# Sparse mixture with TensorE three and six steps behind its row turning

## The chip, the core and the metric

The program runs on one NeuronCore of a Trainium2 chip. Engines are called PE (TensorE matmul; PEld its weight loads), DVE (VectorE), ACT (ScalarE), POOL (GpSimd) and SP (SyncE, which here issues DMAs). The metric is the device time of one execution in microseconds; the median of three runs of the kernel before is 885.31 us (885.22 to 888.61).

## The reference

Two layers of gated cross attention and a gated mixture of experts on 128 x 64 tokens of 128 numbers. The change touches the last mixture alone:

```
h  = layernorm(x)                       # 8192 tokens x 128
i, p = top 2 of 8 experts by h @ Wg     # softmax over the two
out = x + tanh(g) * sum over the two:  p * ((silu(h @ W1[i]) * (h @ W2[i])) @ W3[i])
```

W1 and W2 are 128 x 256, W3 is 256 x 128, for each of 8 experts; all in float32.

## The kernel before

The first phase does the first layer's attention. The second goes in groups of 512 tokens through the first mixture, the second attention and the routing; POOL scatters each normalised row with its share and place to its expert's region in DRAM (`sorted_rows`). The sparse mixture then runs over 135 tiles (`DTILES`) of 128 sorted rows, all of one expert. Its first steps are mixed with the last two groups of the routing, by an order written out by hand.

Each engine has a function `sparse(t)` for step t. No planner sets the order: every engine runs its instructions in the order of the code, and semaphores hold it.

- PE, step t: the first products of tile m = t - HIDDEN (four 128 x 128 products against W1 and W2, line 1938, each float32 product two matmul records), the turning of tile t (line 1948), the output of tile w = t - OUT (two products, line 1957). One signal, `ends_mm`, is given at the end of the step, and `hidden_mm` after the first products.
- ACT, step t: copies the tile's W1 and W2 (`w12`, line 1708) to one of three buffers, then Silu of tile t - HIDDEN (line 1714).
- DVE, step t, once `ends_mm` says that PE's step t is over: the gating product h of tile t - HIDDEN (line 1446, waits for Silu), the copy of the turned tile t to `xT` (line 1451), its two last columns (1452), the share of tile t - OUT (1462), the copy of W3 (1468). From step 86 it also adds 56 pieces of finished groups to X (line 1483).
- POOL, from step 11 on: one indirect DMA for each tile's share (line 1202), each held back until PE's `ends_mm` of a step that the code counts out. Before and between them come the paced scatters of the last two groups' rows (line 1186).
- SP loads the tiles' rows seven ahead (`ROWS`), and later pairs of contributions.

HIDDEN is 2 and OUT is 4. PSUM has eight banks; the first products use banks 0 and 1 in turn, the turned tile bank 3 (from tile 17 on also bank 4), the output banks 5 and 2. So PE's step t needs DVE's step t - 2: its first products wait for `xT` of tile t - 2, which DVE copies after the gating product of tile t - 4.

Of the kernel before, what the change touches and what calls it, by code (L numbers as in the profile page):

```python
# [5 lines left out]
ALU = mybir.AluOpType  # L6
# [7 lines left out]
P = 128  # L14
# [965 lines left out]
def mixtures_and_attention(nc, sb, psum, sem, c, a, X, dispatch, out):  # L980
# [71 lines left out]
    HIDDEN, OUT = 2, 4  # L1052
# [3 lines left out]
    xT = [sb(f"d_xT{i}", [D, P], F32) for i in range(4)]  # L1056
    w12 = [sb(f"d_w12_{i}", [D, 2 * HID1], F32) for i in range(3)]
# [25 lines left out]
    PIECES_AT, FIND_AT = 86, 30  # L1083

    def pair_step(g):
        return 87 + 7 * g // 2
# [7 lines left out]
    found = pair[0:1, 0, 0:2 * LATE_TILES].rearrange("p (k n) -> p k n", k=2)  # L1094
# [19 lines left out]
    with nc.Block() as block:  # L1114
# [115 lines left out]
        def _(dve):  # L1230
# [208 lines left out]
            def sparse(t):  # L1439


                dve.wait_ge(ends_mm, t + 1)
                m = t - HIDDEN
                if 0 <= m < DTILES:
                    dve.wait_ge(silu_done, m + 1)
                    dve.tensor_tensor(d_hidden[m % 4].rearrange("p k n -> p (k n)"), silu[m % 2],  # L1446
                                      uv[m % 2][:, KH * P:2 * KH * P], ALU.mult).then_inc(h_ready, 1)
                if t < DTILES:
                    if t >= 4:
                        dve.wait_ge(hidden_mm, t - 3)  # L1450
                    dve.tensor_copy(xT[t % 4][:], tr_bank(t)[:, 0:P]).then_inc(d_xT_ready, 1)  # L1451
                    dve.tensor_copy(ends[:, t % KEEP, :], rows[t % ROWS][:, D:ROW]).then_inc(row_read, 1)
                w = t - OUT
                if w >= 0:
                    dve.wait_ge(row_read, w + 1)
                    if w % 4 == 0:
                        here = slice(w % KEEP, w % KEEP + min(4, DTILES - w))
                        if w >= KEEP:
                            dve.wait_ge(kept[w // 4 % 8], 64 * (w // KEEP))
                        dve.wait_ge(row_read, min(w + 4, DTILES))  # L1460
                        dve.tensor_copy(token[:, here], ends[:, here, 0])
                    dve.tensor_scalar(shares[w % KEEP], y_bank[w % 2][:, 0:D], ends[:, w % KEEP, 1:2], None,  # L1462
                                      ALU.mult).then_inc(share_ready, 1)
# [118 lines left out]
            for t in range(17, DTILES + OUT):  # L1582
                if t - 18 < dispatch.LATE_STEPS and t >= 18:
                    dispatch.plan_late(dve, c, t - 18, found)
                if t == FIND_AT + 2:
                    dispatch.plan_late(dve, c, dispatch.LATE_STEPS, found)
# [5 lines left out]
        def _(act):  # L1592
# [106 lines left out]
            def sparse(t):  # L1699


                if t < DTILES:
# [3 lines left out]
                    if t >= 3:  # L1706
                        act.wait_ge(hidden_mm, t - 2)
                    act.copy(w12[t % 3][:], c.w12[:, bass.ds(experts[t % 4], 1)].rearrange("d a i h -> d (a i h)")).then_inc(w12_ready, 1)  # L1708
                m = t - HIDDEN
                if m >= 0:  # L1710
                    act.wait_ge(hidden_mm, m + 1)
                    if m >= 2:
                        act.wait_ge(h_ready, m - 1)
                    act.activation(silu[m % 2], uv[m % 2][:, 0:KH * P], ACT.Silu).then_inc(silu_done, 1)  # L1714
# [59 lines left out]
        def _(pe):  # L1774
# [151 lines left out]
            def sparse(t):  # L1926


                m, w = t - HIDDEN, t - OUT
                if 0 <= m < DTILES:  # L1930
                    pe.wait_ge(d_xT_ready, m + 1)
                    pe.wait_ge(w12_ready, m + 1)
                    if m >= 2:
                        pe.wait_ge(h_ready, m - 1)
                    else:
                        pe.wait_ge(k_ready if m == 0 else weighted_ready[0], G)
                    for i in range(2 * KH):
                        last = pe.matmul(uv[m % 2][:, bass.ts(i, P)], w12[m % 3][:, bass.ts(i, P)], xT[m % 4][:], start=True, stop=True)  # L1938
                    last.then_inc(hidden_mm, 1)
                if t < DTILES:  # L1940
# [3 lines left out]
                    elif t == 17:  # L1944
                        pe.wait_ge(next_row_done, G)
                    else:
                        pe.wait_ge(d_xT_ready, t if t <= 16 else t - 1)
                    last = pe.transpose(tr_bank(t)[:, 0:P], rows[t % ROWS][:, 0:D], c.ident[:])  # L1948
                if w >= 0:
                    pe.wait_ge(h_ready, w + 1)  # L1950
                    pe.wait_ge(w3_ready, w + 1)
                    if w >= 2:
                        pe.wait_ge(share_ready, w - 1)
                    else:
                        pe.wait_ge(q_ready if w == 0 else chosen_ready, G - w)
                    for k in range(KH):
                        last = pe.matmul(y_bank[w % 2][:, 0:D], d_hidden[w % 4][:, k, :], w3[w % 8][:, bass.ts(k, D)],  # L1957
# [50 lines left out]
            for t in range(15, DTILES + OUT):  # L2008
                if t == FIND_AT:
                    dispatch.find_late(pe, c, found)  # L2010
# [93 lines left out]
```

## Time and profile before

| what | us |
|---|---|
| median of three runs | 885.31 |
| the profiled execution | 885.49 |
| its span in the profile | 883.7 |
| first to last turning of the sparse mixture | 593.8 to 865.1 |
| last share computed | 871.0 |

PE is busy 766.4 us of the span (87%), DVE 679.8 (77%), ACT 562.8 (64%), POOL 462.4 (52%). These are means over phases with different limits. The sparse mixture takes some 271 us, so it is read by itself: how many matmuls a stretch holds, which waits stand before them, and what the other engines do in those waits. The ends of matmul records are modelled, so a wait of another engine for PE is read from when that other engine starts.

### The profile page before, as it was taken

How to read it: one execution, taken by the hardware profiler on the slowest of the kernel's cores; microseconds unless marked ns; L12 is line 12 of the kernel's file. 1: busy time of each engine (PE TensorE's matmuls, PEld its weight loads, DVE VectorE, ACT ScalarE, POOL GpSimd, SP SyncE). 2: the span in 40 equal slices, each digit the busy share in tenths (PEclk: the TensorE clock that was granted, in tenths of full speed). 3: DMA queues.
4: the chain of work that ended last, by engine and by line, in shares of the span. 5: the costliest groups of instructions: out<-in, count | busy, mean ns of one | idle time of the engine just before them, and what ended most of it. 6: DMA issues, size and time to landing. Idle time of an engine off the chain costs nothing. (4 is left out here: it accounts for less than half of the span.)

```text
span 883.7 us, 26192 instructions
## 1 busy us (share of the span) xinstructions
PE 766.4 (87%) x8321; PEld 589.6 (67%) x8321; DVE 679.8 (77%) x2969; ACT 562.8 (64%) x1195; POOL 462.4 (52%) x498
## 2 busy tenths in 40 slices
PE   4899999999999979989989988757888888889983
PEld 2566666666666646766766755647778777778883
DVE  3889889898898968888888887565466666668984
ACT  2777777777777656888888887444444444445551
POOL 3554344553446011257777776754556565555554
PEclk9999999999999979999999999987799999999997
DMA  9100100001000010011111111211223322357664
GB/s 248 54 23 29 37 21 21 21 23 40 21 21 1 3 41 1 19 34 42 49 46 44 52 42 41 73 37 48 55 75 88 85 74 79 94 156 204 198 185 128
DMA packets 59174, 56.37 MB, mean 64 GB/s; under 512 B 9975, under 2 KB 49176, under 8 KB 59080
## 3 DMA queue, kind: packets, MB, share of 16 engines
q1 hardware_dynamic: 41736, 33.16, 14.2%
q0 software_dynamic: 8416, 17.38, 5.9%
q10 hardware_dynamic: 8928, 4.70, 1.9%
q8 instruction: 44, 0.72, 0.3%
q14 instruction: 50, 0.41, 0.2%
HBM read 32.65 MB, written 22.56 MB: 62 GB/s over the span
## 5 line engine op out<-in xcount | busy, mean ns | idle before, releaser
L1938 PE MATMUL bc_bank<-d_xT,d_w 128*128 128x128 f32 x1080 | 156.6, 290 | 35.1 <-DVE d_xT L1451 26.1
L1202 POOL DMA_INDIRECT contributions<-v_heads,d_token x135 | 132.2, 979 | 99.9 <-PE bc_bank L1957 58.9
L1938 PEld LDWEIGHTS bc_bank<-d_xT,d_w 128*128 128x128 f32 x1080 | 138.6, 201 | 45.0 <-DVE d_xT L1451 33.3
L1186 POOL DMA_INDIRECT sorted_rows<-r_send,r_slots x128 | 126.9, 991 | 48.6 <-issue 39.7
L1714 ACT ACTIVATE b_hidden<-bc_bank 128x256 f32<-128x256 f32 x135 | 51.9, 385 | 140.0 <-PE bc_bank L1938 118.7
L504 POOL TENSOR_SCALAR a_k_heads<-a_kT,first 128x512 f32<-128x512 f32 x60 | 93.2, 1570 | 0.8 <-ACT a_kT L557 0.8
L1708 ACT COPY d_w<-w 128x512 f32 x135 | 82.9, 614 | 5.0 <-issue 2.8
L581 ACT ACTIVATE a_probs<-a_scores 128x1024 f32<-128x1024 f32 x64 | 65.6, 1025 | 29.2 <-PE a_scores L683 29.1
L422 DVE TENSOR_REDUCE a_neg_max<-a_scores 128x16 f32<-128x1024 f32 x64 | 78.1, 1220 | 7.8 <-PE a_scores L673 6.3
L588 ACT COPY a_probsT<-a_probsT_bank 128x512 f32<-128x512 f32 x128 | 74.7, 584 | 13.7 <-PE a_probsT_bank L700 13.2
L700 PE MATMUL a_probsT_bank<-first,a_probs 128*128 128x128 f32 x512 | 80.2, 279 | 2.2 <-ACT a_probsT L588 0.3
L419 DVE TENSOR_REDUCE a_denom<-a_probs 128x16 f32<-128x1024 f32 x64 | 77.4, 1209 | 1.7 <-issue 1.3
L673 PE MATMUL a_scores<-a_k_heads,a_qT 32*64 32x256 f32 x1024 | 70.7, 390 | 2.9 <-issue 2.7
L700 PEld LDWEIGHTS a_probsT_bank<-first,a_probs 128*128 128x128 f32 x512 | 57.9, 142 | 12.5 <-issue 5.8
L495 POOL TENSOR_TENSOR X<-X,out_bias 128x512 f32 (+1 forms) x16 | 20.3, 1270 | 87.0 <-ACT a_xn L544 84.3
L1784 PE MATMUL bc_bank<-b_xnT,w 128*128 128x512 f32 x96 | 51.5, 649 | 12.4 <-ACT c_kT L1633 8.1
L1446 DVE TENSOR_TENSOR b_hidden<-b_hidden,bc_bank 128x256 f32<-128x256 f32 x68 | 28.2, 414 | 43.8 <-ACT b_hidden L1714 21.2
L1446 DVE TENSOR_TENSOR b_weighted<-b_hidden,bc_bank 128x256 f32<-128x256 f32 x67 | 27.8, 415 | 37.4 <-PE bc_bank L1957 19.8
L1948 PE MATMUL bc_bank<-first,d_rows 128*128 128x128 f32 x135 | 38.5, 285 | 9.8 <-DVE d_xT L1451 9.5
L1835 PE MATMUL bc_bank<-w,b_weighted 128*128 128x128 f32 x384 | 46.8, 278 | 0.1
L1462 DVE TENSOR_SCALAR v_heads<-bc_bank,d_ends 128x128 f32<-128x128 f32 x135 | 46.2, 343 | 0.6 <-issue 0.6
L1468 DVE COPY w_in<-w 128x256 f32 x135 | 46.5, 345 | 0.1
(231 smaller groups left out, 1873.6 us busy)
## 6 DMA issues: line engine op xcount, KB each, us to landing
d_rows<-sorted_rows SPq DMA_DIRECT2D x135, 65.0 KB
X<-in_x SPq DMA_DIRECT2D x16, 256.0 KB, 3.1
b_hidden<-contributions SPq DMA_DIRECT2D x8, 512.0 KB
b_weighted<-contributions SPq DMA_DIRECT2D x8, 512.0 KB
out_x<-X ACTq DMA_DIRECT2D x16, 256.0 KB
ctxT<-in_ctx_T SPq DMA_DIRECT2D x16, 192.0 KB, 3.0
c_ctxT<-in_ctx_T SPq DMA_DIRECT2D x16, 192.0 KB
contributions<-v_heads,d_token POOLq DMA_INDIRECT x135
```

What stands on the lines that cost most here:

```text
L419: dve.reduce_sum(denom[:], probs[u % 2][:].rearrange("p (h k) -> p h k", k=S), AX_X).then_inc(sum_done, 1)
L422: dve.tensor_reduce(neg_max[:], scores[u % 2][:].rearrange("p a (h k) -> p (a h) k", k=S), AX_X, ALU.max, negate=True).then_inc(max_done, 1)
L504: last = pool.tensor_scalar(keys_of_head(par, j), kT[:], c.head_of_group[:, j:j + 1], None, ALU.mult)
L581: act.activation(probs[(u + 1) % 2][:], scores[(u + 1) % 2][:].rearrange("p a n -> p (a n)"), ACT.Exp, scale=SCALE0).then_inc(exp_done, 1)
L588: act.copy(probsT[u % 2][:, half * HU // 2:(half + 1) * HU // 2, :].rearrange("p u q -> p (u q)"), probsT_bank[:]).then_inc(pT_ev, 1)
L673: last = pe.matmul(scores[u % 2][S * b:S * b + S, s, bass.ts(h, 4 * S)], qT[par][rows_in, h, tile, :], k_heads[par][rows_in, tile, h].rear ...
L700: last = pe.transpose(probsT_bank[:, bass.ts(k, P)], probs[u % 2][:, bass.ts(half * HU // 2 + k, P)], c.ident[:])
L1186: pool.indirect_dma_start(dispatch.rows, bass.IndirectOffsetOnAxis(ap=slots[n % 2][:, k, j:j + 1], axis=0), send[n % 2][k][:, j, :], None) ...
L1202: pool.indirect_dma_start(dispatch.contributions, bass.IndirectOffsetOnAxis(ap=token[:, t % KEEP:t % KEEP + 1], axis=0), shares[t % KEEP], ...
L1446: dve.tensor_tensor(d_hidden[m % 4].rearrange("p k n -> p (k n)"), silu[m % 2], uv[m % 2][:, KH * P:2 * KH * P], ALU.mult).then_inc(h_read ...
L1708: act.copy(w12[t % 3][:], c.w12[:, bass.ds(experts[t % 4], 1)].rearrange("d a i h -> d (a i h)")).then_inc(w12_ready, 1)
L1938: last = pe.matmul(uv[m % 2][:, bass.ts(i, P)], w12[m % 3][:, bass.ts(i, P)], xT[m % 4][:], start=True, stop=True)
```

## The change

HIDDEN becomes 3 and OUT becomes 6. The first products get four banks in turn (0, 1 and the two of `pair`, from tile 18 on; two before that). The turned tile of a step and the output of the same step share one bank, at different columns: two such banks (3, 5) in turn for steps below 18 (`FIRST`), four (4, 2, 3, 5) from there on. There are five copies of `w12` instead of three, six of `xT` instead of four, four of Silu's result instead of two. PE's waits for a free bank move to the head of the step. DVE copies the turned tile first and does the gating product after it. The late part of the plan (`find_late`, step 30) uses the step's own bank, and DVE reads it in step 30 instead of 32. The steps at which finished groups are fetched and added (`pair_step`, `PIECES_AT`) are 2 later, as the outputs are.

```diff
-    HIDDEN, OUT = 2, 4
+    HIDDEN, OUT = 3, 6
+    W12, TURNED, FIRST = 5, 6, 18
-    silu = tails[0:2]
+    silu = tails[0:2] + tails[6:8]
-    uv, y_bank = bank[0:2], (bank[5], bank[2])
-    def tr_bank(t):
-        return bank[4] if t > 16 and t % 2 else bank[3]
+    def uv(m):
+        return (bank[0], bank[1], pair[:, 0], pair[:, 1])[m % 2 if m < FIRST else (m - FIRST + 2) % 4]
+    def gated_before(m):
+        return m - 4 if m >= FIRST + 2 else m - 2 if m < FIRST else None
+    def step_bank(t):
+        return (bank[3], bank[5])[t % 2] if t < FIRST else (bank[4], bank[2], bank[3], bank[5])[(t - FIRST) % 4]
+    def step_before(t):
+        return t - 2 if t < FIRST else t - 4
+    def y_out(w):
+        return step_bank(w + OUT)[:, P:P + D]
+    def turned(t):
+        return step_bank(t)[:, 0:P]
-    PIECES_AT, FIND_AT = 86, 30
+    PIECES_AT = 88
...
                 dve.wait_ge(ends_mm, t + 1)
+                if t < DTILES:
+                    dve.tensor_copy(xT[t % TURNED][:], turned(t)).then_inc(d_xT_ready, 1)
+                    dve.tensor_copy(ends[:, t % KEEP, :], rows[t % ROWS][:, D:ROW]).then_inc(row_read, 1)
                 m = t - HIDDEN
                 if 0 <= m < DTILES:
                     dve.wait_ge(silu_done, m + 1)
...
-                if t < DTILES:
-                    if t >= 4:
-                        dve.wait_ge(hidden_mm, t - 3)
-                    dve.tensor_copy(xT[t % 4][:], tr_bank(t)[:, 0:P]).then_inc(d_xT_ready, 1)
-                    dve.tensor_copy(ends[:, t % KEEP, :], rows[t % ROWS][:, D:ROW]).then_inc(row_read, 1)
...
-                    if t >= 3:
-                        act.wait_ge(hidden_mm, t - 2)
+                    if t >= W12:
+                        act.wait_ge(hidden_mm, t - W12 + 1)
...
+                before = step_before(t)
+                if before >= 0 and t not in (FIRST, FIRST + 1):
+                    pe.wait_ge(d_xT_ready, min(before + 1, DTILES))
+                    if before >= OUT:
+                        pe.wait_ge(share_ready, before - OUT + 1)
+                if t == FIND_AT:
+                    dispatch.find_late(pe, c, found)
                 if 0 <= m < DTILES:
                     pe.wait_ge(d_xT_ready, m + 1)
                     pe.wait_ge(w12_ready, m + 1)
-                    if m >= 2:
-                        pe.wait_ge(h_ready, m - 1)
-                    else:
+                    if m < 2:
                         pe.wait_ge(k_ready if m == 0 else weighted_ready[0], G)
+                    elif gated_before(m) is not None:
+                        pe.wait_ge(h_ready, gated_before(m) + 1)
...
-                    else:
-                        pe.wait_ge(d_xT_ready, t if t <= 16 else t - 1)
-                    last = pe.transpose(tr_bank(t)[:, 0:P], rows[t % ROWS][:, 0:D], c.ident[:])
+                    last = pe.transpose(turned(t), rows[t % ROWS][:, 0:D], c.ident[:])
...
-                    if w >= 2:
-                        pe.wait_ge(share_ready, w - 1)
```

The order on PE in steps 33 and 34, before. `d_xT3` is a buffer with its number; the names in brackets are the semaphores waited for.

```order
L1938 MATMUL bc_bank1<-d_xT3,d_w12_1 128x128 [waits d_h_ready,d_w12_ready,d_xT_ready]
L1938 MATMUL bc_bank1<-d_xT3,d_w12_1 128x128 x3
L1948 MATMUL bc_bank4<-first,d_rows5 128x128 [waits d_xT_ready,d_loaded5]
L1957 MATMUL bc_bank2<-w3_in,b_hidden1 128x128 [waits d_share,d_w3_ready,d_h_ready]
L1957 MATMUL bc_bank2<-w3_in,b_hidden1 128x128
L1938 MATMUL bc_bank0<-d_xT0,d_w12_2 128x128 [waits d_h_ready,d_w12_ready,d_xT_ready]
```

The same step 33 and the head of 34 on PE, now:

```order
L1962 MATMUL bc_pair<-d_xT0,d_w12_0 128x128 x3
L1974 MATMUL bc_bank5<-first,d_rows5 128x128 [waits d_loaded5]
L1979 MATMUL bc_bank5<-w3_in,b_weighted0 128x128 [waits d_w3_ready,d_h_ready]
L1979 MATMUL bc_bank5<-w3_in,b_weighted0 128x128
L1962 MATMUL bc_pair<-d_xT1,d_w12_1 128x128 [waits d_w12_ready,d_xT_ready,d_h_ready,d_share]
```

The kinds and their number are the same; the tile of the first products is 30 where it was 31, that of the output 27 where it was 29, turned tile and output stand in one bank, and the waits for a free bank stand at the head of the step.

The order on DVE in step 33 before, and the first rows of step 34:

```order
L1446 TENSOR_TENSOR b_weighted0<-b_hidden0,bc_bank1 128x256 [waits d_silu_done,d_ends_mm]
L1451 COPY d_xT1<-bc_bank4 128x128 [waits d_hidden_mm]
L1452 COPY d_ends<-d_rows5 128x2
L1462 TENSOR_SCALAR v_heads1<-bc_bank2,d_ends 128x128 [waits d_row_read]
L1468 ISA
L1468 COPY w3_in<-w3 128x256
L1446 TENSOR_TENSOR b_hidden1<-b_hidden0,bc_bank0 128x256 [waits d_silu_done,d_ends_mm]
```

And now:

```order
L1463 COPY d_xT3<-bc_bank5 128x128 [waits d_ends_mm]
L1464 COPY d_ends<-d_rows5 128x2
L1468 TENSOR_TENSOR b_weighted0<-b_weighted1,bc_pair 128x256 [waits d_silu_done]
L1481 TENSOR_SCALAR v_heads1<-bc_bank5,d_ends 128x128 [waits d_row_read]
L1487 ISA
L1487 COPY w3_in<-w3 128x256
```

The copy to `xT` no longer stands behind the gating product and its wait for Silu, nor does it wait for `hidden_mm`.

## Rows read from the trace of the kernel before

**Rows 1.** Windows: busy us (instructions) of each engine, PE clock, DMA share, GB/s.

```profile
core 0: us, PE busy (x) PEld busy (x) DVE busy (x) ACT busy (x) POOL busy (x), PEclk, DMA share, GB/s
593.00:643.00 50.00, 39.43 (x260) 37.51 (x261) 26.18 (x141) 23.52 (x53) 25.20 (x31) 0.76 0.19 51
655.00:777.00 122.00, 102.81 (x845) 97.07 (x843) 78.66 (x342) 56.18 (x126) 70.32 (x73) 0.99 0.32 86
787.00:866.00 79.00, 68.87 (x571) 65.12 (x570) 66.63 (x279) 40.31 (x88) 44.48 (x45) 1.00 0.65 185
```

**Rows 2.** Windows of line 1938 alone: PE busy (matmuls), PEld busy (loads), clock, DMA.

```profile
643.00:655.00 12.00, 5.73 (x39) 5.31 (x39) 0.94 0.28 67
655.00:777.00 122.00, 71.75 (x516) 62.82 (x514) 0.99 0.32 86
777.00:787.00 10.00, 5.85 (x37) 5.41 (x38) 0.83 0.45 149
787.00:866.00 79.00, 48.47 (x351) 42.29 (x350) 1.00 0.65 185
```

**Rows 3.** Timeline, PE: start, us, operation, count; two steps without a wait.

```profile
659.65 1.06 PE L1938 MATMUL bc_bank<-d_xT,d_w 128*128 128x128 f32 x8
661.10 1.06 PE L1938 MATMUL bc_bank<-d_xT,d_w 128*128 128x128 f32 x8
```

**Rows 4.** Waits in 655 to 777: total us, times, longest.

```profile
ACT b_hidden L1714 <- PE bc_bank L1938: 57.6, 41, 3.7
POOL contributions L1202 <- PE bc_bank L1957: 34.0, 25, 1.8
PEld bc_bank L1938 <- DVE d_xT L1451: 17.6, 16, 1.9
PEld bc_bank L1938 <- issue: 6.5, 10, 0.9
```

**Rows 5.** Timeline, 683 to 689, one long wait; in brackets the idle time before.

```profile
683.03 1.06 PE L1938 MATMUL bc_bank<-d_xT,d_w 128*128 128x128 f32 x8
684.06 0.96 POOL L1202 DMA_INDIRECT contributions<-v_heads,d_token  x1 [0.30 <-issue]
685.03 1.16 PE L1938 MATMUL bc_bank<-d_xT,d_w 128*128 128x128 f32 x8 [0.38 <-issue]
685.32 1.00 POOL L1202 DMA_INDIRECT contributions<-v_heads,d_token  x1 [0.30 <-issue]
687.26 0.38 ACT L1714 ACTIVATE b_hidden<-bc_bank 128x256 f32<-128x256 f32 x1 [3.69 <-PE bc_bank L1938]
687.75 0.42 DVE L1446 TENSOR_TENSOR b_hidden<-b_hidden,bc_bank 128x256 f32<-128x256 f32 x1 [2.25 <-ACT b_hidden L1714]
688.05 0.96 POOL L1202 DMA_INDIRECT contributions<-v_heads,d_token  x1 [1.73 <-PE bc_bank L1957]
688.09 0.28 DVE L1451 COPY d_xT<-bc_bank 128x128 f32<-128x128 f32 x1
688.43 0.82 PE L1938 MATMUL bc_bank<-d_xT,d_w 128*128 128x128 f32 x5 [1.69 <-DVE d_xT L1451]
```

**Rows 6.** Timeline, DVE: a whole step that adds a piece, without a wait.

```profile
825.11 0.41 DVE L1446 TENSOR_TENSOR b_hidden<-b_hidden,bc_bank 128x256 f32<-128x256 f32 x1
826.17 0.42 DVE L1483 TENSOR_TENSOR X<-X,b_weighted 128x256 f32<-128x256 f32 x1
826.50 0.41 DVE L1446 TENSOR_TENSOR b_weighted<-b_hidden,bc_bank 128x256 f32<-128x256 f32 x1
```

**Rows 7.** Timeline, PE, 779 to 784: after a wait of 1.89 us.

```profile
779.00 1.35 PE L1938 MATMUL bc_bank<-d_xT,d_w 128*128 128x128 f32 x8 [1.89 <-DVE d_xT L1451]
780.15 0.42 PE L1948 MATMUL bc_bank<-first,d_rows 128*128 128x128 f32 x1
782.92 0.42 PE L1948 MATMUL bc_bank<-first,d_rows 128*128 128x128 f32 x1
```

**Rows 8.** Waits in 590 to 643: total us, times, longest.

```profile
PE bc_bank L1948 <- DVE d_xT L1451: 9.5, 6, 4.0
```

**Rows 9.** Timeline of the end: the last shares, their DMAs, the last addition.

```profile
870.67 0.35 DVE L1462 TENSOR_SCALAR v_heads<-bc_bank,d_ends 128x128 f32<-128x128 f32 x1 [0.56 <-issue]
874.02 0.96 POOL L1202 DMA_INDIRECT contributions<-v_heads,d_token  x1 [0.31 <-issue]
880.26 0.69 DVE L1491 TENSOR_TENSOR X<-X,b_weighted 128x512 f32<-128x512 f32 x1
```

More of the change, by code:

```diff
@@ L1055, in mixtures_and_attention @@
     rows = [sb(f"d_rows{i}", [P, ROW], F32) for i in range(ROWS)]
-    xT = [sb(f"d_xT{i}", [D, P], F32) for i in range(4)]
-    w12 = [sb(f"d_w12_{i}", [D, 2 * HID1], F32) for i in range(3)]
+    xT = [sb(f"d_xT{i}", [D, P], F32) for i in range(TURNED)]
+    w12 = [sb(f"d_w12_{i}", [D, 2 * HID1], F32) for i in range(W12)]
     w3 = [c.w3_in[:].rearrange("p e k d -> p e (k d)")[:, i] for i in range(8)]
     tails = [b[:, C0 - 1, i * KH * P:(i + 1) * KH * P] for b in hidden + weighted for i in range(2)]
-    silu = tails[0:2]
+    silu = tails[0:2] + tails[6:8]
     d_hidden = [b.rearrange("p (k n) -> p k n", k=KH) for b in tails[2:6]]
@@ L1082, in mixtures_and_attention @@
     PIECES = 4 * CLOSED
[L1083 removed]
+    PIECES_AT = 88
     def pair_step(g):
[L1086 removed]
+        return 89 + 7 * g // 2
     def piece_step(i):
@@ L1092, in store_step @@
         return piece_step(4 * g + 3) + 4
-    found = pair[0:1, 0, 0:2 * LATE_TILES].rearrange("p (k n) -> p k n", k=2)
     def blocks_kept(eng, blocks):
@@ L1461, in sparse @@
                         dve.tensor_copy(token[:, here], ends[:, here, 0])
-                    dve.tensor_scalar(shares[w % KEEP], y_bank[w % 2][:, 0:D], ends[:, w % KEEP, 1:2], None,
+                    dve.tensor_scalar(shares[w % KEEP], y_out(w), ends[:, w % KEEP, 1:2], None,
                                       ALU.mult).then_inc(share_ready, 1)
@@ L1705, in sparse @@
                         experts[:] = dispatch.four_tiles(mybir.EngineType.Activation, dispatch.tile_expert, t, E1 - 1)
-                    if t >= 3:
-                        act.wait_ge(hidden_mm, t - 2)
-                    act.copy(w12[t % 3][:], c.w12[:, bass.ds(experts[t % 4], 1)].rearrange("d a i h -> d (a i h)")).then_inc(w12_ready, 1)
+                    if t >= W12:
+                        act.wait_ge(hidden_mm, t - W12 + 1)
+                    act.copy(w12[t % W12][:], c.w12[:, bass.ds(experts[t % 4], 1)].rearrange("d a i h -> d (a i h)")).then_inc(w12_ready, 1)
                 m = t - HIDDEN
@@ L1711, in sparse @@
                     act.wait_ge(hidden_mm, m + 1)
-                    if m >= 2:
-                        act.wait_ge(h_ready, m - 1)
-                    act.activation(silu[m % 2], uv[m % 2][:, 0:KH * P], ACT.Silu).then_inc(silu_done, 1)
+                    if m >= 4:
+                        act.wait_ge(h_ready, m - 3)
+                    act.activation(silu[m % 4], uv(m)[:, 0:KH * P], ACT.Silu).then_inc(silu_done, 1)
                 for g in range(CLOSED):
@@ L1932, in sparse @@
                     pe.wait_ge(w12_ready, m + 1)
-                    if m >= 2:
-                        pe.wait_ge(h_ready, m - 1)
-                    else:
+                    if m < 2:
                         pe.wait_ge(k_ready if m == 0 else weighted_ready[0], G)
+                    elif gated_before(m) is not None:
+                        pe.wait_ge(h_ready, gated_before(m) + 1)
                     for i in range(2 * KH):
-                        last = pe.matmul(uv[m % 2][:, bass.ts(i, P)], w12[m % 3][:, bass.ts(i, P)], xT[m % 4][:], start=True, stop=True)
+                        last = pe.matmul(uv(m)[:, bass.ts(i, P)], w12[m % W12][:, bass.ts(i, P)], xT[m % TURNED][:], start=True, stop=True)
                     last.then_inc(hidden_mm, 1)
@@ L1943, in sparse @@
                         pe.wait_ge(v_ready, G)
-                    elif t == 17:
+                    elif t == 1:
+                        pe.wait_ge(q_ready, G)
+                    elif t == FIRST:
                         pe.wait_ge(next_row_done, G)
-                    else:
-                        pe.wait_ge(d_xT_ready, t if t <= 16 else t - 1)
-                    last = pe.transpose(tr_bank(t)[:, 0:P], rows[t % ROWS][:, 0:D], c.ident[:])
+                    elif t == FIRST + 1:
+                        pe.wait_ge(chosen_ready, G)
+                    last = pe.transpose(turned(t), rows[t % ROWS][:, 0:D], c.ident[:])
                 if w >= 0:
@@ L1951, in sparse @@
                     pe.wait_ge(w3_ready, w + 1)
-                    if w >= 2:
-                        pe.wait_ge(share_ready, w - 1)
-                    else:
-                        pe.wait_ge(q_ready if w == 0 else chosen_ready, G - w)
                     for k in range(KH):
-                        last = pe.matmul(y_bank[w % 2][:, 0:D], d_hidden[w % 4][:, k, :], w3[w % 8][:, bass.ts(k, D)],
+                        last = pe.matmul(y_out(w), d_hidden[w % 4][:, k, :], w3[w % 8][:, bass.ts(k, D)],
                                          start=(k == 0), stop=(k == KH - 1))
```

12 lines of the change are left out of this document (6 added, 6 removed).

## The prediction

> **What bounds the kernel now.** I read the windows first, since the sparse mixture is a phase of its own and the only one that the change touches. In 655 to 777, PE is busy 102.8 of 122 us, at a granted clock of 0.99 (its 2.4 GHz level), and no other engine comes near: DVE 78.7, POOL 70.3, ACT 56.2 [rows 1]. Each step issues eight matmul records of the first products, so the 516 records there are 64.5 steps, and a step takes 122 / 64.5 = 1.89 us; in 787 to 866 it is 351 / 8 = 43.9 steps of 1.80 us [rows 2]. Where PE waits for nothing, one step follows the other after 1.45 us (661.10 less 659.65) [rows 3]. PE is the bound, but each step loses 0.35 to 0.44 us.
>
> The waits say to what. PE's weight loads for the first products stood 17.6 us for DVE's copy to `xT` and 6.5 us for nothing that is shown [rows 4]. Behind that stands a wait the other way: ACT waited 57.6 us for PE's first products, up to 3.7 us, and POOL 34.0 us for the ends of steps [rows 4]. The timeline of one such case shows what the reader is to see [rows 5]: the first products begun at 683.03 are over at 684.09 by the records, but Silu, which waits for them, starts at 687.26, 3.17 us later, though ACT had been idle for 3.69 us. Meanwhile PE ran its next step (685.03) and then had to stop, since step t needs DVE's step t - 2. After the release the chain is Silu, gating product (687.75), copy to `xT` (688.09), first products (688.43): 1.17 us. PE's idle time before them is 1.69 us. So the signals of PE's ends come late, in groups, and two steps of lead don't cover it. In these delays POOL issues its indirect DMAs one right behind the other (684.06 and 685.32, 1.26 apart), and the signals come back 1.94 us after the start of the last one. I take it that the two belong together; the trace shows only that they fall together.
>
> The Trainium skill, page Perfetto Trace Analysis, section Tensor Engine Instruction, says that the end of a matmul record is an estimate from its size, and that the signal is sent only when PSUM has acknowledged all bytes. The trace agrees that a record's end is no proof of a signal: 3.17 us lie between [rows 5]. By the page PE might really have been late there; the sum would be the same, since it uses the readers' starts.
>
> **The change part by part.** No instruction is added or removed; PE's step keeps its 13 matmul pairs. What changes is the lead.
>
> (a) Lead of three steps, and the copy to `xT` first. In the case of rows 5, the copy would follow the step's end signal at once instead of behind Silu and the gating product: some 0.4 us after the release (0.28 of copy and some 0.1), not 1.17. And PE would need it one step, 1.45 us, later. 1.69 - 1.45 - 0.77 is below zero: the wait is gone, if the delay stays as long as it was. The gating product is next needed by the output at the end of the third step, 0.4 + 2 x 1.45 + 1.0 = 4.3 us after the first products; 3.17 + 0.38 (Silu) + 0.42 fit in. So one end is 1.45 us a step.
> The other end: the delays may grow with the lead. A case with n of POOL's DMAs in a row takes (n - 1) x 1.26 + 1.94 until the release and 0.79 until POOL starts again (688.05 less 687.26) [rows 5]. For n = 2 that is 3.99 us or 2.0 a step; for n = 3, which a lead of three steps allows, 5.25 us or 1.75 a step. Now 1.89 is a mixture of 80% at 2.0 and 20% at 1.45; with 1.75 it would be 1.69. So in 655 to 777 the gain is between 64.5 x 0.20 = 13 and 64.5 x 0.44 = 28 us. I take 18 (a step of 1.61), nearer the lower end, because the case with POOL is what rows 5 show.
> In 787 to 866 the mixture is 64% and 36%: between 43.9 x 0.16 = 7 and 43.9 x 0.35 = 15 us. DVE, which adds pieces there, needs 1.39 us for a step (826.50 less 825.11) [rows 6], just under PE's 1.45, so the lower end again: 8 us.
> The 22 us of 643 to 655 and 777 to 787 hold 76 / 8 = 9.5 steps [rows 2], 8 us more than 1.45 each; between 2 and 8, I take 4.
>
> (b) The first 18 steps. 128 records, 16 steps, in 50 us (593 to 643), at a clock of 0.76 [rows 1]. Up to step 16 the turning waits for the copy of the tile just before it, and stood 9.5 us for that [rows 8]; now it waits for the one two before. But the groups of routing stand between, and POOL's scatters are tied to the steps. Between 0 and 9.5; I take 4.
>
> (c) More buffers (five `w12`, six `xT`, four Silu) cost nothing: there is no instruction more, and the waits for them are met earlier. Moving the waits for a bank to the head of the step costs nothing either: they ask for DVE's step t - 4, while the first products ask for t - 3. In steps below 18 they ask for t - 2, as now. The reading of the late plan in step 30 is 2 steps earlier and stays on DVE; it saves or costs under 0.5 us. The fetches on SP's queue and the additions on DVE for finished groups come 2 steps later, as the shares that they need do; behind them on their queues stand the same instructions as before.
>
> (d) Two more steps at the end. They hold only an output each, but the last tile's Silu and gating product are then uncovered, as they are now. The last share is ready at 870.67 + 0.35 and POOL's last DMA starts at 874.02, with three still to issue [rows 9]; the tail behind (landing, one pair, additions, store) is untouched. Between 0 and 3 us lost; I take 1.
>
> Sum: 18 + 8 + 4 + 4 - 1 = 33 us. The profiled execution took 885.49 (span 883.7), 0.2 above the median of the runs, so 885.3 - 33 = 852 us. The ends of the terms are 13 + 7 + 2 + 0 - 3 = 19 (866) and 28 + 15 + 8 + 9.5 = 60 (825).
>
> **Rivals.** All of the lead pays: the delays keep their length and PE runs through at 1.45 to 1.5. For it: (a). Against: POOL would have to issue every 1.26 of 1.45 us, and DVE 1.39 of 1.45. 28 + 12 + 7 + 6 - 1 = 52, so 833 us.
>
> The delays eat the lead: the signals come by POOL's runs alone, whose length grows with the steps that are outstanding, and a step costs 1.80 instead of 1.89 in the middle. For it: POOL waited for a step's end 25 times in these 64.5 steps [rows 4], so late signals are common. Against: runs of three at 1.75 are the worst that rows 5 give. 64.5 x 0.09 + 43.9 x 0.05 + 2 + 2 - 1 = 11, so 874 us.
>
> Nothing: POOL's own pace is counted in PE's steps, and if its handshake sets the pace (2.0 us for a run of two, whatever PE could do), it stays 885 us. Against: steps of 1.45 follow each other where it is quiet.
>
> Slower: fewer but longer waits at PE. After 1.89 us of waiting the step from 780.15 to 782.92 took 2.77 us instead of 1.45, with records of 0.42 instead of 0.27 [rows 7]: the 1.2 GHz level, in a stretch whose clock is 0.83 [rows 2]. The wait of 1.69 us before 688.43 had none behind it (5 records in 0.82) [rows 5]. If runs of three DMAs make each wait 3 us or longer, then one in seven steps (16 of 117) would be followed by 1.3 us at that level, with the present loss kept: 16 x 1.3 + 1 = 22, less 4 at the front, 903 us. It decides as soon as PE's waits are regularly over 1.9 us. Against: the change makes waits shorter in every case that I can work out.
> The Trainium skill, page TensorE: Matmul & The Clock Gate, section What's actually happening, says the same rule: the array idles at 1.2 GHz and activity releases it. The trace agrees, with records of 0.42 after the wait [rows 7]; by that rule alone a smoother PE would gain at the front too, where the clock is 0.76.
>
> **How the numbers follow.** Forecast (844 to 866 around 852) 0.50. Full gain (under 844, 833) 0.20. Delays eat the lead (866 to 881, 874) 0.17. Nothing 0.05. Slower 0.08. The range 832 to 880 leaves out about 2 in 10: the lower end of the full gain (0.08), and nothing and slower (0.13). A change of 0.5%, 4.4 us, is about what can be told from none: faster 0.87, same 0.05, slower 0.08.
>
> **What would show it.** Right: the windows of the middle hold a step every 1.55 to 1.7 us, PE's waits for `xT` fall from 17.6 us to under 8, and the late part has DVE over 90% busy. If the signals stay as late as now, Silu still starts up to 3 us behind the records, but PE does not stop. POOL's DMAs in rows of three would show the lower end. Wrong: a middle step of 1.80 or more with PE waiting for `xT` as before, or records of 0.42 in the middle. A front of 50 us as now would make (b) nothing; over 5 us more between the last turning and the last share would make (d) wrong.

## The result and the profile after

The changed kernel takes 873.64 us (median of four runs, 869.87 to 876.62) against 886.28 before: ratio 0.9863, 95% interval 0.9831 to 0.9895. It is faster by 1.4%, as foreseen in sign, but the gain is 12.6 us and not 33. A second series of the same kernel gave 871.86 (0.9857, 0.9829 to 0.9885). Of the cases, "the delays eat the lead" (874 us) is the one that came.

The profiled execution took 876.62 us, its span 874.8. A step is read as in the prediction: eight records of the first products (now line 1962) a step. Below, the windows of the changed kernel, first all engines, then line 1962 alone; they answer to [rows 1, 2].

```profile
598.00:646.00 48.00, 34.35 (x244) 32.72 (x240) 26.84 (x147) 23.42 (x52) 26.42 (x32) 0.82 0.21 55
654.00:767.00 113.00, 101.83 (x835) 97.70 (x835) 72.94 (x343) 53.33 (x128) 67.43 (x70) 0.97 0.32 84
778.00:849.00 71.00, 66.95 (x552) 64.81 (x553) 64.08 (x273) 37.28 (x88) 42.07 (x42) 0.98 0.70 204
```

```profile
654.00:767.00 113.00, 70.71 (x511) 64.02 (x511) 0.97 0.32 84
778.00:849.00 71.00, 47.39 (x342) 42.49 (x343) 0.98 0.70 204
```

The middle holds 511 / 8 = 63.9 steps in 113 us: 1.77 us each, where 1.89 was and 1.61 was forecast. The late part has 71 / 42.75 = 1.66 against 1.80. The clock of the middle fell from 0.99 to 0.97.

The waits of the changed kernel, 654 to 767 (engine, line, tile waited for: us in total, times, longest), answer to [rows 4]; line 1731 is Silu, 1221 POOL's share, 1463 the copy to `xT`, 1979 the output:

```profile
ACT b_weighted L1731 <- PE bc_bank L1962: 37.9, 11, 4.5
POOL contributions L1221 <- PE bc_bank L1979: 23.2, 14, 1.9
POOL contributions L1221 <- issue: 16.7, 51, 0.8
ACT b_weighted L1731 <- remote: 14.7, 6, 4.7
PEld bc_bank L1962 <- DVE d_xT L1463: 10.1, 11, 2.0
PE bc_bank L1962 <- DVE d_xT L1463: 7.0, 6, 1.7
```

ACT waits less often, but up to 4.7 us and not 3.7: the late signals became later. PE's loads for the first products stood 10.1 us for `xT` where it was 17.6; the 7.0 us of the matmuls belong to the same stops. POOL was held by PE 14 times and not 25: between turnings 22 and 86, 49 of its 69 DMAs start less than 0.45 us after the one before, where 38 of 72 did. The timeline shows one case; it answers to [rows 5].

```profile
682.21 0.96 POOL L1221 DMA_INDIRECT contributions<-v_heads,d_token  x1 [1.77 <-PE bc_bank L1979]
683.47 0.96 POOL L1221 DMA_INDIRECT contributions<-v_heads,d_token  x1 [0.30 <-issue]
683.50 1.06 PE L1962 MATMUL bc_pair<-d_xT,d_w 128*128 128x128 f32 x8
684.74 1.00 POOL L1221 DMA_INDIRECT contributions<-v_heads,d_token  x1 [0.30 <-issue]
684.95 1.06 PE L1962 MATMUL bc_pair<-d_xT,d_w 128*128 128x128 f32 x8
686.04 0.96 POOL L1221 DMA_INDIRECT contributions<-v_heads,d_token  x1 [0.30 <-issue]
686.40 1.06 PE L1962 MATMUL bc_bank<-d_xT,d_w 128*128 128x128 f32 x8
687.31 0.96 POOL L1221 DMA_INDIRECT contributions<-v_heads,d_token  x1 [0.31 <-issue]
689.38 0.38 ACT L1731 ACTIVATE b_weighted<-bc_pair 128x256 f32<-128x256 f32 x1 [4.69 <-remote]
689.45 0.29 DVE L1463 COPY d_xT<-bc_bank 128x128 f32<-128x128 f32 x1 [3.49 <-PE bc_bank L1979]
689.96 1.95 PE L1962 MATMUL bc_bank<-d_xT,d_w 128*128 128x128 f32 x8 [1.03 <-DVE d_xT L1463]
```

POOL issues five DMAs in a row. Rows 5 show two, but these were the last two of a run of four. The first two stand just ahead of them in the trace of the kernel before:

```profile
681.53 0.96 POOL L1202 DMA_INDIRECT contributions<-v_heads,d_token  x1 [1.35 <-PE bc_bank L1957]
682.79 0.96 POOL L1202 DMA_INDIRECT contributions<-v_heads,d_token  x1 [0.30 <-issue]
```

In the changed kernel, the first products over at 684.56 reach Silu at 689.38. PE runs its three steps of lead and stops all the same; then the eight records take 1.95 us and not 1.06, most of them at the 1.2 GHz level (granted clock 0.65 in 689 to 692.5). The chain behind the release did shrink, from 1.17 to 0.58 us (689.38 to 689.96), since the copy no longer stands behind Silu and gating.

The end, answering to [rows 9] (1481 the last share, 1508 and 1510 the last additions):

```profile
856.99 2.12 PE L1979 MATMUL bc_bank<-w_in,b_hidden 128*128 128x128 f32 x8 [1.89 <-DVE v_heads L1481]
859.73 0.96 POOL L1221 DMA_INDIRECT contributions<-v_heads,d_token  x1 [0.30 <-DVE v_heads L1481]
860.07 0.35 DVE L1481 TENSOR_SCALAR v_heads<-bc_bank,d_ends 128x128 f32<-128x128 f32 x1 [0.58 <-PE bc_bank L1979]
865.17 0.96 POOL L1221 DMA_INDIRECT contributions<-v_heads,d_token  x1 [0.30 <-issue]
870.66 0.69 DVE L1508 TENSOR_TENSOR X<-X,b_weighted 128x512 f32<-128x512 f32 x1 [8.44 <-DMA b_weighted<-contributions]
871.39 0.69 DVE L1510 TENSOR_TENSOR X<-X,b_weighted 128x512 f32<-128x512 f32 x1
```

POOL's last DMA starts 5.1 us behind the last share's start, 3.35 before. Between the last turning and the end of the span lie 25.5 us, 18.5 before.

The turnings' starts make the balance of the spans (883.7 to 874.8, 8.9 us): steps 0 to 18 gained 3.2, 18 to 22 gained 2.4, 22 to 86 gained 7.5, 86 to 134 gained 7.1, the tail lost 7.0, and the mixture began 4.3 later. That last item is not the change's: in the second series the first turning came at 593.5 us, against 593.8 before and 598.1 here, and the span was 869.0. Over all the traces of this document it lies between 592.7 and 598.9, in edits of either kernel. Without it the gain is 13.

### The profile page after: what moved, and what is told of

It reads as the page before. It is cut to its first block and busy times, and to the rows that moved or that the text cites. A ratio compares the mean times of both kernels' runs of the same rounds, so it can differ in the third digit from the quotient of the medians.

```text
span 874.8 us, 26065 instructions
## 1 busy us (share of the span) xinstructions
PE 769.0 (88%) x8321; PEld 592.6 (68%) x8321; DVE 672.8 (77%) x2969; ACT 555.9 (64%) x1195; POOL 462.9 (53%) x498
## 5 line engine op out<-in xcount | busy, mean ns | idle before, releaser
L1962 PE MATMUL bc_bank<-d_xT,d_w 128*128 128x128 f32 x608 | 88.6, 291 | 21.8 <-DVE d_xT L1463 9.6
L1962 PEld LDWEIGHTS bc_bank<-d_xT,d_w 128*128 128x128 f32 x608 | 78.9, 202 | 26.7 <-DVE d_xT L1463 23.8
L1463 DVE COPY d_xT<-bc_bank 128x128 f32<-128x128 f32 x135 | 38.3, 284 | 68.5 <-PE bc_bank L1979 53.4
L422 DVE TENSOR_REDUCE a_neg_max<-a_scores 128x16 f32<-128x1024 f32 x64 | 78.1, 1221 | 10.6 <-PE a_scores L673 9.2
L673 PE MATMUL a_scores<-a_k_heads,a_qT 32*64 32x256 f32 x1024 | 72.6, 399 | 2.9 <-issue 2.7
L1731 ACT ACTIVATE b_weighted<-bc_pair 128x256 f32<-128x256 f32 x59 | 22.8, 387 | 72.2 <-PE bc_bank L1962 43.7
L1962 PE MATMUL bc_pair<-d_xT,d_w 128*128 128x128 f32 x472 | 65.0, 282 | 0.6 <-issue 0.5
L1731 ACT ACTIVATE b_hidden<-bc_bank 128x256 f32<-128x256 f32 x68 | 26.7, 393 | 53.7 <-PE bc_pair L1962 25.8
L1962 PEld LDWEIGHTS bc_pair<-d_xT,d_w 128*128 128x128 f32 x472 | 59.5, 198 | 1.5 <-issue 0.9
L1979 PE MATMUL bc_bank<-w_in,b_hidden 128*128 128x128 f32 x272 | 46.1, 285 | 6.1 <-issue 3.8
L673 PEld LDWEIGHTS a_scores<-a_k_heads,a_qT 32*64 32x64 f32 x1024 | 33.8, 135 | 20.1 <-issue 10.8
```

The source lines that it names most:

```text
L422: dve.tensor_reduce(neg_max[:], scores[u % 2][:].rearrange("p a (h k) -> p (a h) k", k=S), AX_X, ALU.max, negate=True).then_inc(max_done, 1)
L673: last = pe.matmul(scores[u % 2][S * b:S * b + S, s, bass.ts(h, 4 * S)], qT[par][rows_in, h, tile, :], k_heads[par][rows_in, tile, h].rear ...
L1962: last = pe.matmul(uv(m)[:, bass.ts(i, P)], w12[m % W12][:, bass.ts(i, P)], xT[m % TURNED][:], start=True, stop=True)
```

## The experiments

Two quantities below are worked out from the traces. "Lateness" is the time from the modelled end of a tile's last first-product record to the start of its Silu, over tiles 22 to 133. Silu can't start before the signal `hidden_mm`, so no signal is later than that; ACT's own queue is in it where several signals come at once. (The signals' own records can't give it for every tile, since about one in ten is missing from the traces.) A "run" is a row of POOL's DMAs with less than 0.45 us between them. In the middle, the kernel before has runs of 2.1 DMAs, the changed one runs of 3.5 (3.9 in the second series); the mean lateness is 0.73 us before (longest 3.2) and 2.06 us in the changed kernel (longest 4.8).

### Are POOL's indirect DMAs the cause?

```diff
-                pool.indirect_dma_start(dispatch.contributions, bass.IndirectOffsetOnAxis(ap=token[:, t % KEEP:t % KEEP + 1], axis=0),
-                                        shares[t % KEEP], None).then_inc(kept[t // 4 % 8], 16)
+                pool.dma_start(dispatch.contributions[bass.ts(t, P), :], shares[t % KEEP]).then_inc(kept[t // 4 % 8], 16)
```

> The changed kernel, with POOL storing each of the 135 shares by a plain DMA (row t*128 on) in place of the indirect one; the combination then reads rows of other tokens, the work is the same in number and bytes. Theory A (PE's completion signals are held back while POOL works off indirect DMAs, and the remaining 0.3 us a step are those): the steps of the middle (turnings 22 to 86, now 1.77 us each) and of the late part (86 to 134, 1.70) take 1.45 to 1.50, Silu starts within 0.2 us of its records everywhere, POOL no longer hangs behind at the end (5 us): 840 us or less. Theory B (PE's signals are late by themselves, or through DVE's and ACT's own work): the steps stay above 1.65 and the time within 1% of 873.

> The same edit in the kernel before (leads of 2 and 4). Theory A: without late signals a lead of two is enough, steps of 1.45 to 1.55, so within 1.5% of the changed kernel with plain DMAs, under 850 us. Theory B: steps stay at 1.85 to 1.9, about 885 us.

Measured: 833.0 us (0.9413, 0.9375 to 0.9451) and 835.96 (0.9431, 0.9391 to 0.947). Theory A holds: steps, time and the end come out as it says. The changed kernel with plain DMAs, all engines in the middle and late part, and two rows of its timeline:

```profile
650.00:741.00 91.00, 91.00 (x817) 90.74 (x817) 74.64 (x342) 57.26 (x126) 37.63 (x70) 1.00 0.38 106
748.00:810.00 62.00, 62.00 (x558) 62.00 (x557) 62.00 (x272) 39.99 (x86) 23.67 (x44) 1.00 0.83 239
```

```profile
690.62 1.06 PE L1961 MATMUL bc_bank<-d_xT,d_w 128*128 128x128 f32 x8
691.71 0.38 ACT L1730 ACTIVATE b_hidden<-bc_bank 128x256 f32<-128x256 f32 x1 [0.56 <-PE bc_bank L1961]
```

PE never stops, a step is 1.45 us, and Silu starts 0.03 us behind the records here. The mean lateness is 0.05 us; it is over 0.2 for three tiles (0.5 at most). PE's signals, where the trace has them, come at most 0.02 us behind the records. PE, and in the late part DVE beside it, is busy throughout. With prompt signals the kernel before is within 3 us of the changed one: a lead of two is enough then.

This run also holds its own comparison. The scatters of the routing are still indirect DMAs in it, and seven of them stand in a row from 617.98 to 626.5 us. In that stretch PE's signals are as late as ever: first products whose records end at 622.49 reach Silu at 628.06.

```profile
621.35 1.14 PE L1961 MATMUL bc_bank<-d_xT,d_w 128*128 128x128 f32 x8
628.06 0.38 ACT L1730 ACTIVATE b_hidden<-bc_bank 128x256 f32<-128x256 f32 x1 [4.78 <-remote]
```

To tell the kind of DMA from the time that POOL is busy, each share went as two plain DMAs:

```diff
+                for h in range(2):
+                    half = slice(64 * h, 64 * h + 64)
+                    pool.dma_start(dispatch.contributions[t * P + 64 * h:t * P + 64 * h + 64, :], shares[t % KEEP][half, :]).then_inc(kept[t // 4 % 8], 16)
```

> The changed kernel with each share stored by two plain DMAs of 64 rows (to rows of other tokens, as with one plain DMA), so that POOL is busy 2 x 0.54 us and two gaps a step, as long as with one indirect DMA (0.99 and a gap). Theory A (it is the indirect DMA that holds PE's signals back): steps of 1.45, about 833 us. Theory A' (any equally busy POOL does it): steps of 1.6 or more as in the changed kernel, over 860.

A single run took 836.53 us. POOL's row in 650 to 875 and the first products of the middle:

```profile
L1223 POOL DMA_DIRECT2D contributions<-v_heads x258 | 138.6, 543 | 35.6 <-issue 27.1 <-PE bc_bank L1980 6.5 <-DVE v_heads L1482 1.2
```

```profile
650.00:741.00 91.00, 65.97 (x500) 60.83 (x501) 1.00 0.42 102
```

POOL is busier than with the indirect DMAs (129 of 986 ns, 127.2 us, from 654 on in the changed kernel), and 500 / 8 = 62.5 steps take 91 us, 1.46 each. Up to 94 of these plain DMAs stand in a row with less than 0.45 us between them, and no recorded signal is more than 0.02 us behind. So it is the indirect DMA and not a busy POOL. The plain DMAs also write to rows of DRAM that lie one behind the other, where the indirect ones scatter them; the two were not taken apart. Why the indirect DMA holds PE's signals back no run here shows.

### The parts of the change

`order_first` is the kernel before with the copy to `xT` moved ahead of the gating product; `order_last` is the changed kernel with it moved back:

```diff
+                    dve.tensor_copy(xT[t % 4][:], tr_bank(t)[:, 0:P]).then_inc(d_xT_ready, 1)
...
                 if 0 <= m < DTILES:
                     dve.wait_ge(silu_done, m + 1)
...
-                    dve.tensor_copy(xT[t % 4][:], tr_bank(t)[:, 0:P]).then_inc(d_xT_ready, 1)
```

> The kernel before, with one part of the change alone: DVE copies xT ahead of the gating product. Theory A1 (a late signal's price is the chain behind its release, 1.17 us of which 0.77 goes): PE's 16 waits for xT in the middle lose up to 0.77 us each, 12 us, and half as much late: 868 to 875 us, so most of what the whole change gave. Theory A2 (the signals come by POOL's runs alone, and what is saved behind one is waited for at the next): under 4 us, 882 to 886.

> The changed kernel with the gating product ahead of the xT copy, as it was before: the longer lead alone. A1: it is the order that pays, so 880 or more. A2: the longer lead pays and the order does not: 871 to 877, as the changed kernel.

Measured: 883.06 (0.9965, 0.9944 to 0.9986) and 876.59 (0.9883, 0.9851 to 0.9915). A2 is right. The order alone brings 3 us, though its chain shrank; lead and buffers alone bring 10.

```diff
-    HIDDEN, OUT = 3, 6
+    HIDDEN, OUT = 2, 4      # lead24
+    HIDDEN, OUT = 4, 6      # hidden4
```

> The changed kernel with the leads of before (first products 2 steps behind the turning, outputs 4), so that what is left of the change is the order on DVE, the buffers, the banks and the waits. If these count for nothing, it is the kernel before with the xT copy first: 883 (that one took 883.06), the late signals as short as there (mean run of POOL's DMAs 2.1). If the buffers and the waits on older steps pay by themselves: 878 or less.

> The changed kernel once more, on the chip of the three beside it, so that the parts are compared with it there: 870 to 877. If the 3.7 us by which its profiled run reached the sparse mixture later than the kernel before belong to the change, they are there again; if not, the first turning comes at 594 to 596 us.

> The changed kernel with first products 4 steps behind the turning and not 3, the outputs 6 behind as now, all buffers as now. A1 (what a late signal costs is PE's wait for xT, 17 us in the middle; more lead there takes it away): steps of 1.70 in the middle, 5 to 8 us gained, 866. A2 (the delays take any lead, since POOL's runs end only when PE has stopped): 870 to 877, with the waits moved to the output (h_ready, share). Slower, if the two steps left for Silu and gating are too short for a late signal: 880.

`lead24` took 879.05 (0.9936, 0.9907 to 0.9965), and the changed kernel beside it 871.86. So the leads are worth 7 us. Order and buffers together are worth 6; that the buffers do more than the order alone stays within the intervals. `hidden4` took 877.61 (0.9896, 0.9873 to 0.992), not faster. Its mean lateness fell to 1.32 us, with 4.4 for the longest, yet the steps of 22 to 86 took 1.82 us. With two steps left between first products and output the wait moved there: in 654 to 767 PE's loads for the output stood 18.1 us for the gating product.

### POOL's pacing

```diff
-                keep_share(t, t + OUT + 1 + max(0, 10 - (t - 6) // 8))
+                keep_share(t, t + OUT)                                                       # ungated
+                keep_share(t, t + OUT + 1 + 10 - (t - 6) // 8 if t < 86 else t + OUT)        # ungated_late
```

(The step asked for is then one that the share itself needs, so it holds nothing.)

> The changed kernel, in which POOL stores a share as soon as it is there, without waiting for a PE step (lag of up to 11 steps in the changed kernel, falling to 1). Theory A with the run length as the price, (n - 1) x 1.26 + 1.94 us: at the start some ten shares are waiting, POOL runs through them in 12 us and PE stands for most of that, once; after it POOL follows share by share in short runs: 64 x 0.1 gained, 10 lost, so 865 to 885. If runs do not matter and only the number of DMAs does: 873 or less, since the same 129 DMAs are issued, and the last one comes right behind the last share.

> The changed kernel with the pacing taken away for tiles 86 to 134 alone, where it asks for one PE step behind the share. A: POOL starts a share 1.15 us earlier and is less far behind at the end (5.1 us there now): 2 to 4 us gained, 870. If POOL's runs of 1.27 us a share are what bounds the tail, the last DMA comes no earlier: 873 or 874.

Measured: 881.86 (0.9942, 0.9918 to 0.9967) and 877.15 (0.9892, 0.987 to 0.9913). In `ungated` POOL issued 13 share DMAs in a row from 654.18 to 669.86. ACT's Silu meanwhile:

```profile
657.41 0.38 ACT L1731 ACTIVATE b_hidden<-bc_bank 128x256 f32<-128x256 f32 x1 [3.89 <-PE bc_pair L1962]
664.58 0.38 ACT L1731 ACTIVATE b_hidden<-bc_bank 128x256 f32<-128x256 f32 x1 [5.78 <-remote]
673.08 0.38 ACT L1731 ACTIVATE b_weighted<-bc_pair 128x256 f32<-128x256 f32 x1 [7.61 <-PE bc_bank L1962]
```

In 655 to 676 PE's first products have 37 records, under five steps in 21 us. That is the price of a long run: 16.6 us more for the steps 26 to 30 than at 1.45. Behind it, 676 to 776 holds 464 records, 1.72 us a step. Letting go of the pacing late brought nothing, and may have lost 3 us: POOL still ended 4.1 us behind.

When does a pending signal get out? Over the seven traces with indirect DMAs up to here I took each pause of POOL behind a DMA during which a signal of PE was due. In pauses of 0.3 us one got out 17 times in 399, of 0.6 to 0.8 us 25 times in 49, of 0.9 us or more 251 times in 252. It mostly comes out 0.4 to 1.1 us after the DMA's end. Two things weaken this count. Since some signals lack a record, it depends on how the rest are paired (another pairing gives 50 in 568, 25 in 54 and 247 in 247). And four in five of the pauses of 0.9 us or more ended because POOL had waited for such a signal, so that they can't but hold one. A fair test needs pauses that end by themselves. So POOL was given pauses, by clearing a region that nothing reads any more:

```diff
+                keep_share(t, t + OUT)
+                if t % 3 == 2:                                    # pause3; t % 2 == 1 in pause2
+                    pool.wait_ge(numbered, G + quiets)
+                    pool.memset(w_padded[:].rearrange("p t n -> p (t n)"), 0.0).then_inc(numbered, 1)
+                    quiets += 1
```

> The changed kernel in which POOL doesn't wait for PE's steps, but after every third share clears a region that nothing reads any more (128x512, some 0.5 us), so that it is quiet for some 0.9 us there. In the traces so far a pending signal of PE got out in 17 of 399 pauses of 0.3 us, in 25 of 49 of 0.6 to 0.8 and in all of 0.9 us or more. If that is the rule, no delay passes 3 x 1.27 + 1 us, the ten shares that wait at the start don't block PE (ungated lost 17 us there), and the steps take 1.45 to 1.6: 855 to 868. If the end of a POOL run is not what lets the signals out, it is ungated with more POOL work: 880 or more.

> The same with a pause after every second share. Delays end by 3.5 us, which the lead covers wholly, but POOL needs (2 x 1.27 + 0.6) / 2 = 1.57 us a share: steps of 1.57 once its backlog counts, so 870 to 880 by that rule; near pause3 if POOL's pace is not felt.

Measured: 878.54 (0.9919, 0.9894 to 0.9944) and 873.12 (0.9848, 0.9815 to 0.9881). The pause came out mostly at 0.70 to 0.87 us and not 0.9; three of POOL's rows in `pause2` show one of 0.84:

```profile
658.88 0.68 POOL L1249 MEMSET b_w_padded<- 128x512 bf16 x1
659.73 0.96 POOL L1221 DMA_INDIRECT contributions<-v_heads,d_token  x1 [0.17 <-PE bc_bank L1984]
661.00 0.96 POOL L1221 DMA_INDIRECT contributions<-v_heads,d_token  x1 [0.30 <-issue]
```

Of the 55 such pauses with a signal due, in both kernels together, 42 let one out. So a pause that POOL makes by itself does release signals, but not every time, and `pause3` fails its forecast of 855 to 868. `pause2` meets the rule's 870 to 880: with pauses after every second DMA the first ten shares cost 13 us over seven steps (29 to 35), and the steps of 86 to 134 take 1.61 us, against 1.67 to 1.70. POOL is then the one that is late: its last DMA starts 6.5 us behind the last share. Behind the first ten shares both are quicker than the changed kernel with its 1.78 us a step: 1.67 in `pause3` (turnings 25 to 80) and 1.64 in `pause2` (36 to 86). Not all of that is the pauses', since POOL issues one DMA a step there and not nine in eight, and `ungated` had 1.72 without them. From its first share DMA after 650 to its last, POOL takes 1.62 to 1.65 us a DMA in the changed kernel, `ungated_late`, `order_last`, `hidden4` and `pause2` alike, and 1.71 in the kernel before. As all of them issue the same 129 DMAs, this says that their loops take the same time; it doesn't show that POOL sets it.

```diff
+                keep_share(t, t + OUT + 1 + (10 if t < 86 else 0))        # even, before_even
```

> The changed kernel with POOL's lag kept at 11 steps for tiles 6 to 85, so that it issues one share a step in the middle and not nine in eight steps; what it has put off comes in one run at tile 86. Only the middle (turnings 25 to 80) is to be read; the burst afterwards costs some 15 us, as in ungated. If a step costs POOL's cycle (runs of 3.5 to 3.9 DMAs of 1.27 us and a pause of 1.5 to 1.6, divided by the steps that they belong to), the middle takes 1.68 to 1.71 us a step in place of 1.78. If the catching up is hidden: 1.78 as now.

> The kernel before with the same even lag (11 steps for tiles 6 to 85), again only for its middle, turnings 25 to 80, which took 1.90 us a step before. If each DMA less is worth what it was worth in the changed kernel (1.78 to 1.60 for one ninth fewer), it is 1.72, and the leads' part of the change is 0.12 there as here; if the lead of two is what binds it, it stays at 1.85 to 1.90 and the longer lead would have been worth 0.25 or more without the catching up.

The first products of the middle, first `even`, then `before_even`, then the kernel before for the same tiles:

```profile
654.00:742.00 88.00, 59.29 (x445) 53.81 (x444) 1.00 0.36 91
```

```profile
658.00:755.00 97.00, 61.79 (x448) 54.13 (x447) 1.00 0.31 82
```

```profile
661.00:764.00 103.00, 59.99 (x432) 52.39 (x432) 1.00 0.30 81
```

In steps from turning 25 to 80: 1.595 us in `even` against 1.78, and 1.747 in `before_even` against 1.90. `even` is below the 1.68 to 1.71 expected (the cycle it was worked out from is too dear), `before_even` close to its 1.72. One ninth fewer DMAs is worth 0.185 and 0.153 us a step, 1.2 to 1.5 us for each DMA left out. The lead is worth 0.12 with the catching up and 0.15 without. As whole kernels both are no gain (878.6 and 890.94 us, a single run each), since what was put off comes in runs of ten: the two stops near steps 90 and 107 took 8.0 and 10.9 us at their longest.

> The changed kernel with its own pacing up to tile 85, and from there to tile 117 shares stored as they come with a pause of 0.7 us after every second one (the late part took 1.61 us a step with such pauses, 1.67 to 1.70 without). Steps 86 to 134 gain 3 us, POOL ends at most 1 us later: 869 to 871, just below the changed kernel. If the shorter late part is given back by POOL's lag at the end (6.5 us with pauses throughout): 873 or more.

```diff
+                keep_share(t, t + OUT + 11 - (t - 6) // 8 if t < 86 else t + OUT)
+                if t % 2 == 1 and 86 <= t < 118:                                  # the pause of pause2
```

875.47 us (0.9876, 0.985 to 0.9902), steps of 1.73 from 86 on: the late gain of `pause2` did not come again, so I can't claim that it was the pauses. No version with the whole computation beats the changed kernel; `pause2` equals it.

## Why the prediction was right in sign and wrong in size

**What bounds the kernel.** Right as far as it went: PE loses its time to late signals, and they belong to POOL's indirect DMAs. What only fell together in [rows 5] is now shown by taking the DMAs' kind away. PE was called the bound; with indirect DMAs POOL's instructions count as much, since each one more in the loop costs 1.2 to 1.5 us.

**(a) The lead.** This step failed, by 10 of 18 us in the middle: 1.77 us a step for 1.61. Two things were wrong in it.

First, the length of POOL's runs: "for n = 2", and "n = 3, which a lead of three steps allows". The case of rows 5 was itself a run of four, and six of the 34 runs between turnings 22 and 86 of the kernel before had four. In the changed kernel 13 of 20 have four or five, with 86% of the DMAs. It is the same at one DMA a step: the mean run is 1.9 in `before_even` and 3.2 in `even`. So the delays grew with the lead beyond what the sum allowed, and its lower end of 0.20 us a step was no floor.

Second, and larger, the sum gave each step one DMA, while the pacing makes POOL issue nine in eight steps up to tile 86 (between turnings 22 and 86 it is 72 DMAs before and 69 after, some scatters coming first). `before_even` and `even` take just this away, and steps of 1.90 and 1.78 us become 1.747 and 1.595. Thus 0.15 us of each step before was the price of the ninth DMA (0.19 in the changed kernel), and the sum counted it as loss that the lead could take. On what is left the lead brought 0.15 us a step and not the forecast's 0.28, and with the ninth DMA 0.12. That 1.595 lies so near to the forecast's 1.61 is in part chance, for 1.61 was chosen between 1.45 and 1.69. The pacing stands in the code of POOL's loop, as a lag of 10 that falls by one every eight tiles; I had read it as a delay and not as a rate. In the changed kernel POOL's time between these turnings is 67 us of DMAs, 15 us of short gaps and 28.5 us in 19 longer pauses, 110 of 113 us.

PE's waits for `xT`, read at the loads as in the forecast, fell from 17.6 us to 10.1 and not to under 8 (at the matmuls from 14.6 to 7.0); in `even` they are 3.2. In the late part 7.1 us were gained (8 forecast), and the four steps of 18 to 22, about half of the stretches for which the sum took 4, gained 2.4.

**(b) The first 18 steps.** Right: 3.2 us, 3.5 in the second series, for 4.

**(c) Buffers and waits.** They were put at nothing; `lead24` is 2.6 us below `order_first` by their ratios, and the intervals overlap, so it stays open.

**(d) The end.** Wrong in size, 7 us lost for 1 (0 to 3 allowed). The runs with plain DMAs show what the two steps cost by themselves. From the last turning to the end of the span it is 18 us with the long leads (span 829.7) and 16 with the short ones (span 833.6), so 2 us:

```profile
811.79 0.27 PE L1973 MATMUL bc_bank<-first,d_rows 128*128 128x128 f32 x1
817.72 0.27 PE L1947 MATMUL bc_bank<-first,d_rows 128*128 128x128 f32 x1
```

The other 5 us come with the indirect DMAs. PE waits 1.89 us for a share's bank in the last steps. The last six shares then come within 3.4 us (856.65 to 860.07), where POOL needs 1.26 to 1.65 us for each, so it is 5.1 us behind at the end and not 3.35. How the 5 us divide between these is not shown.

**The rivals.** "The delays eat the lead" has the right mechanism, but held runs of three to be the worst, and its time is right partly by luck: it gave 2 us to the late part (7.1 measured) and 1 us lost to the end (7), and the two misses cancel. "Fewer but longer waits at PE" was partly there: three steps of 3.2 to 4.4 us had one of 2.3 to 2.8 behind, in part at the 1.2 GHz level. That is 3.5 us, not 22. "Full gain" is near what both kernels do without the indirect DMAs (833.0 and 836 us); that its 833 is met to the digit is chance, since it was added up for a kernel with them.

## What to carry to other kernels

Before you lengthen a lead to cover a late signal, find what ends the delay. If it is a pause of another engine, a longer lead makes that engine's runs longer and the delay with them. Count that engine's instructions per step from the code that paces them, and price the step with the engine's own cycle; work put off into the loop costs there what it costs the loop, here 1.2 to 1.5 us for each DMA of 1.27. And steps added at a pipeline's end are not free, even if almost nothing is in them: here 2 us for two with prompt signals, and 7 us with late ones.

## What the runs showed of the hardware

While POOL works off indirect DMAs of 128 rows (0.96 us each, 0.30 between), PE's completion signals arrive up to 4.8 us late (`hidden_mm`, changed kernel, tiles 22 to 133), and mostly come out in a pause of POOL, 0.4 to 1.1 us after a DMA's end, then 0.07 to 0.09 us apart. PE itself runs on meanwhile, but not quite freely: its loads stood still for nothing that is shown for 6.5 us in the middle before and 4.7 us in the changed kernel, and never with plain DMAs. DVE's signals showed no such delay: before, PE started 0.06 us after the end of a copy to `xT` in all 29 cases in which it waited and the copy ended inside an indirect DMA of POOL. In a run of 13 DMAs some still got out, one in 2 to 5 us. POOL's plain DMAs, one or two a share, delay nothing (0.02 us at most). Another way to issue the indirect ones was not tried.

The Trainium skill, page TensorE: Matmul & The Clock Gate, section The cost: per-tile semaphore tail, gives some 26 ns for each increment where the matmuls of several tiles signal one after another. No run here has that case. The traces with plain DMAs agree that a signal of PE costs little (0.02 us at most behind the modelled end); with indirect DMAs it came up to 4.8 us late, which no such figure covers, and the measurement decides.
